# A graph-attention and residual-norm kernel: row maxima of every third chunk subtracted by an accumulating DMA, and the maxima written and read in another layout

## The chip, the cores and the metric

The kernel runs on one core of one Trainium2 chip. The metric is the device time of one execution in microseconds (us). Three executions of the kernel before took 1765.34, 1768.12 and 1771.2 us, median 1768.12 us. A fourth was recorded by the profiler; all rows below come from it. PE is TensorE, PEld its weight loads, DVE is VectorE, ACT is ScalarE, POOL is GpSimd, SP is SyncE; "SPq" and "POOLq" are the instructions with which these two start DMAs.

## What is computed

Eight graphs of 1500 nodes with 64 features pass through four layers, each followed by a residual addition and a layer norm. The change touches only the first layer, a graph attention with four heads:

```python
scores = jnp.einsum('hbnd,hbdm->hbnm', f_self, f_other)
masked = a_h * scores
masked = jnp.where(masked >= 0, masked, 0.2 * masked)
masked = masked / jnp.sqrt(jnp.float32(ATT))
masked = masked + jnp.where(a_h == 0, jnp.float32(-1000000000.0), jnp.float32(0.0))
attn = jax.nn.softmax(masked, axis=-1)
attn = attn * jnp.where(a_h == 0, jnp.float32(0.0), jnp.float32(1.0))
...
node_features = jnp.einsum('bhnm,bhmo->bhno', attn, feats)
```

The softmax needs the maximum over m of each row n, which is subtracted before the exponential. The other three layers multiply the adjacency matrix with the features (a mean over neighbours, a dense layer, a thresholded sum).

## The kernel before

**Units and chunks.** A graph's attention is cut into 6 units (2 pairs of heads times 3 slices of 500 rows n). In a unit the scores stand transposed, m on the partitions and n along the row, in 12 chunks (`STEPS`) of 125 partitions x 1000 numbers (two heads x 500 rows n). There are 48 units and 576 chunks. All engines walk through one common counter `q` of chunks, each executing what its list has for that `q`; semaphores hold them together.

**One chunk q.** PE fills a bank pair of the 3-deep ring `Z` with mask and scores (`fill_z`, lines 496 and 498), and may do so only when the ring's user three places earlier has been read. ACT applies the leaky slope and writes the chunk to the row store `LS` (`bend`, line 677), DVE folds it into the running maximum `RUN` straight from `Z` (`maximum`, lines 820 and 823). Since the maximum is known only when all 12 chunks are through, the rest follows `LAG` = 18 chunks later: chunk e = q - 18 gets its maxima subtracted, ACT exponentiates it at q = e + 20 (`expo`, line 685), and PE weighs it, two chunks at a time, at e + 22 (`weigh`, line 535).

**The subtraction.** Of each three chunks (`TURN`) POOL subtracts two (line 403) and DVE the third (line 837), as the last thing in DVE's list for that `q`. They take turns: before the first of its two, POOL waits on `sub_dve` until DVE has done the chunk before. POOL's list also has the loads of the adjacency matrix (line 365, a DMA that casts f32 to fp8), the power of the layer norms (408), the low halves (412) and the bases of the later layers (417, 420).

**The maxima's way.** At the unit's end PE transposes `RUN` (`turn_run`, line 509, eight transposes, each reading 125 columns of `RUN` with a stride of `ST` = 4 elements), DVE reduces (line 829), ACT applies the slope (line 692), SP writes 125 x 8 numbers to the HBM buffer `row_maxima` as 125 x 2 runs of 4 (line 303), waits for that, and reads them back, broadcast to 125 partitions of `MB` (line 309). `MB` has two halves, one per unit in turn.

**Layer norms and the later layers** of graph b - 1 run beside the attention of graph b: DVE has six larger operations a layer (among them lines 905, 909, 914 and 922), ACT squares and casts, PE multiplies the adjacency matrix (line 586) and turns the result back (line 596). After the last attention chunk these stages of graph 7 run alone.

## Time and profile before

| | |
|---|---|
| median of three executions | 1768.12 us |
| the profiled execution, whole | 1762.62 us |
| its span, first to last instruction | 1760.8 us |
| PE busy | 1454.2 us (83%) |
| DVE busy | 1384.5 us (79%) |
| ACT busy | 1241.6 us (71%) |
| POOL busy | 1089.5 us (62%) |
| mean granted clock of TensorE | 0.912 of 2.4 GHz |

The profiled execution took 5.5 us less than the median. The first read of the maxima starts at 89.0 us and the last at 1649.2 us, so 47 unit intervals take 1560.2 us, 33.2 us each, or 2.77 us a chunk; 89 us lie ahead of them and 112 us behind. In the profile, "idle before" an instruction is the time for which its engine stood still, and the name behind the arrow is what ended that. A mean busy time of a pipelined matmul is shorter than its own duration, because neighbours overlap.

### The profile page before, as it was taken

To read this page: it belongs to the slowest core of one execution; us is meant where nothing else is said; L and a number is where in the kernel's file an instruction comes from. 1 tells how busy PE (TensorE), PEld (TensorE's weight loads), DVE (VectorE), ACT (ScalarE), POOL (GpSimd) and SP (SyncE) were. 2 spreads that over 40 slices of the span, in tenths; PEclk is the share of its full clock that TensorE was granted. 3 is DMA by queue.
4 is the path that set the end of the run, shared out by engine and by line. 5 is a ranking of instruction groups with operands and counts; after the bars stand their busy time and mean duration, and the time that the engine had idled before them with its cause. 6 is when DMAs were issued, how large, how long until landed. Compare 5 with 4: busy or idle time off the path is not lost.

```text
span 1760.8 us, 22052 instructions
## 1 busy us (share of the span) xinstructions
PE 1454.2 (83%) x7728; PEld 718.8 (41%) x7728; DVE 1384.5 (79%) x1623; ACT 1241.6 (71%) x1475; POOL 1089.5 (62%) x581
## 2 busy tenths in 40 slices
PE   4487889898889889888889888988899987888745
PEld 3233334444444444444444443444444443344313
DVE  3567788878898778888888778987888788888654
ACT  2377878777687777777787777777687777777521
POOL 1056676676676666676576667776666766766642
PEclk9788989999899999999999999999999999999767
DMA  5413142122413133221522234130432214000000
GB/s 77 61 32 48 31 66 40 46 30 39 70 31 46 26 52 51 52 36 26 68 40 43 25 55 58 39 44 17 63 46 52 30 37 55 21 12 24 15 6 9
DMA packets 55067, 71.42 MB, mean 41 GB/s; under 512 B 21814, under 2 KB 42814, under 8 KB 54958
## 3 DMA queue, kind: packets, MB, share of 16 engines
q0 software_dynamic: 13824, 18.01, 13.7%
q1 hardware_dynamic: 41134, 52.01, 11.4%
q8 instruction: 62, 1.02, 0.3%
q14 instruction: 47, 0.39, 0.1%
HBM read 102.29 MB, written 3.26 MB: 60 GB/s over the span
## 4 chain that ended last, share of the span: by engine, by line
PE 45%; DVE 24%; issue 12%; ACT 11%; SPq 3%; POOL 3%; DMA 2%; ACTq 0%; POOLq 0%; DVEq 0%
PE M L586 11%; DVE RUN L823 9%; PE M L535 9%; PE Z L496 8%; PE Z L498 7%; ACT LS L677 6%; PE Z L509 4%; DVE LS L837 4%; ACT LS L685 3%; SPq L286 2%; DVE X L922 2%; POOL LS L403 2%; PE Z L596 2%; DVE RUN L820 2%; PE Z L657 2%
## 5 line engine op out<-in xcount | busy, mean ns | idle before, releaser
L403 POOL TENSOR_TENSOR LS<-LS,MB 125x1000 f32<-125x1000 f32 x384 | 894.7, 2346 | 489.4 <-DVE LS L837 334.8
L823 DVE TENSOR_TENSOR RUN<-Z,RUN 125x1000 f32<-125x1000 f32 x528 | 631.0, 1195 | 208.7 <-ACT LS L677 203.4
L677 ACT ACTIVATE LS<-Z 125x1000 f32<-125x1000 f32 x576 | 574.5, 998 | 262.0 <-PE Z L498 261.4
L685 ACT ACTIVATE LS<-LS 125x1000 f32<-125x1000 f32 x576 | 594.5, 1033 | 71.3 <-POOL LS L403 56.2
L496 PE MATMUL Z<-AT,BI 126*125 126x500 fp8e4 x1152 | 386.0, 418 | 140.1 <-DVE RUN L823 107.0
L535 PE MATMUL M<-LS,V 125*18 125x500 f32 x2304 | 326.7, 642 | 57.8 <-ACT LS L685 57.0
L498 PE MATMUL Z<-FS,FO 96*125 96x500 bf16 x1152 | 360.1, 395 | 0.0
L837 DVE TENSOR_TENSOR LS<-LS,MB 125x1000 f32<-125x1000 f32 x192 | 283.2, 1475 | 4.9 <-DMA MB<-row_maxima 2.8
L496 PEld LDWEIGHTS Z<-AT,BI 126*125 126x125 bf16 x1152 | 140.7, 146 | 282.9 <-DVE RUN L823 164.5
L498 PEld LDWEIGHTS Z<-FS,FO 96*125 96x125 bf16 x1152 | 165.5, 144 | 111.4 <-issue 21.3
L586 PE MATMUL M<-AT,XP 125*128 125x500 fp8e4 x756 | 206.8, 396 | 0.7 <-ACTq L735 0.7
L586 PEld LDWEIGHTS M<-AT,XP 125*128 125x128 f16 x756 | 63.6, 98 | 169.6 <-issue 106.8
L509 PE MATMUL Z<-ID,RUN 125*125 125x125 f32 x384 | 99.9, 407 | 26.8 <-DVE RUN L820 24.1
L535 PEld LDWEIGHTS M<-LS,V 125*18 125x18 f32 x2304 | 39.6, 98 | 185.4 <-issue 101.7
L509 PEld LDWEIGHTS Z<-ID,RUN 125*125 125x125 f32 x384 | 91.5, 323 | 46.3 <-DVE RUN L820 39.9
L365 POOL DMA_DIRECT2D A<-in_adj_dram x96 | 53.7, 560 | 85.9 <-PE Z L552 58.7
L820 DVE TENSOR_SCALAR RUN<-Z 125x1000 f32<-125x1000 f32 x48 | 57.3, 1193 | 47.8 <-DMA B<-in_L_gnn_bias_dram 30.0
L829 DVE TENSOR_REDUCE RMAX<-Z 125x8 f32<-125x1000 f32 x48 | 57.3, 1194 | 26.1 <-PE Z L509 26.1
L596 PEld LDWEIGHTS Z<-WW,YT 128*125 128x125 f32 x504 | 63.9, 190 | 28.7 <-issue 22.0
L922 DVE SCALAR_TENSOR_TENSOR X<-Y,RSTD 125x768 f32<-125x768 f32 x28 | 72.4, 2585 | 3.6 <-POOL RSTD L408 2.4
L596 PE MATMUL Z<-WW,YT 128*125 128x64 f32 x504 | 64.7, 272 | 3.7 <-DVE RUN L820 3.7
L552 PEld LDWEIGHTS Z<-ID,A 125*125 125x125 f32 x276 | 45.8, 215 | 53.5 <-issue 28.5
(118 smaller groups left out, 1039.6 us busy)
## 6 DMA issues: line engine op xcount, KB each, us to landing
MB<-row_maxima SPq DMA_DIRECT2D x48, 488.3 KB
A<-in_adj_dram POOLq DMA_DIRECT2D x96, 183.1 KB, 4.8
FO<-PARTS SPq DMA_DIRECT2D x192, 46.9 KB, 2.1
FS<-PARTS SPq DMA_DIRECT2D x192, 46.9 KB, 2.1
XP<-in_x_dram SPq DMA_DIRECT2D x8, 375.0 KB
XA<-in_x_dram SPq DMA_DIRECT2D x8, 375.0 KB
out_dram<-X SPq DMA_DIRECT2D x7, 375.0 KB
row_maxima<-LMAX SPq DMA_DIRECT2D x48, 3.9 KB
```

The source lines that it names most:

```text
L403: nc.gpsimd.tensor_tensor(rows, rows, MB[:, u % 2, :, :], ALU.subtract).then_inc(sub_pool, 1)
L496: nc.tensor.matmul(z[:P, hh, :], BI[:, :], AT[:, g % RS, quarter, :, k], start=True, stop=False)
L498: last = nc.tensor.matmul(z[:P, hh, :], FO[:, 2 * p + hh, m * P:(m + 1) * P], FS[:, 2 * p + hh, s * C:(s + 1) * C], start=False, stop=True)
L509: last = nc.tensor.transpose(z[:P, hh, c * P:(c + 1) * P], RUN[:, u % 2, hh, c:C:ST], ID[:P, :P])
L535: last = nc.tensor.matmul(M0[VW * n:VW * n + VC, 0:C], V[:, b % 2, e % STEPS, 2 * p + hh, :], LS[:P, e % RL, hh, :], start=(p == 1 and j = ...
L586: last = nc.tensor.matmul(M1[:, 0:C], XP[:, m, :], AT[:P, (NS * b + c) % RS, m // ST, :, m % ST], start=(m == 0), stop=(m == NT - 1))
L596: last = nc.tensor.matmul(z[:P, 0, k * F:(k + 1) * F], YT[:, k * P:(k + 1) * P], WW[:, 1 if l == 1 else 0, :], start=True, stop=True)
L677: nc.scalar.activation(LS[:P, q % RL, :, :], banks("Z", q)[:P], ACT.Prelu, alpha=0.2).then_inc(bent, 1)
L685: nc.scalar.activation(rows, rows, ACT.Exp, scale=0.25).then_inc(exps, 1)
L823: nc.vector.tensor_tensor(run, z, run, ALU.max).then_inc(maxed, 1)
L837: nc.vector.tensor_tensor(rows, rows, MB[:, u % 2, :, :], ALU.subtract).then_inc(sub_dve, 1)
L922: nc.vector.scalar_tensor_tensor(out=X[:, :, :], in0=Y[:, :, :], scalar=F ** 0.5, in1=RSTD[:, :].unsqueeze(2).to_broadcast(bc3), op0=ALU.m ...
```

## The change

Five things change.

1. Every third chunk (c % 3 = 2 within its unit) is no longer subtracted by DVE. POOL starts a DMA from `MB` to `LS` that accumulates (`accum_op=ALU.add`) for chunk e + 2 ahead of its own subtraction of chunk e, so 192 DMAs of 125 x 1000 f32 in all. ACT's `expo` of such a chunk waits for that DMA's semaphore, one of four (`BY_DMA`).
2. POOL keeps its two of three, and no longer waits for a turn.
3. ACT now makes the negative of the maximum (`scale=-0.2, alpha=5.0`), and both POOL and the DMA add it.
4. PE's transposes read `RUN` in contiguous blocks of 125 columns in place of every fourth column. The maxima then lie as (j i) and are written as 1000 pieces of one number, by two DMAs of 112 and 13 partitions.
5. `MB` has 128 partitions, and the broadcast read fills all 128.

```diff
-                sp.dma_start(spread[u % 2].rearrange("(h i c) -> i h c", i=P, c=ST),
-                             LMAX[:, u % 2, :].rearrange("p (h c) -> p h c", c=ST)).then_inc(max_out[u % 2], 16)
-                sp.wait_ge(max_out[u % 2], 16 * (u // 2 + 1))
+
+                for rows in (slice(0, 112), slice(112, P)):
+                    sp.dma_start(spread[u % 2].rearrange("(j i) -> i j", i=P)[rows], LMAX[rows, u % 2, :],
+                                 allow_slow_non_contiguous=True).then_inc(max_out[u % 2], 16)
+                sp.wait_ge(max_out[u % 2], 32 * (u // 2 + 1))
                 if u >= 2:
-                    sp.wait_ge(sub_pool, by_pool(STEPS * (u - 1)))
-                    sp.wait_ge(sub_dve, STEPS * (u - 1) // TURN)
+
+                    sp.wait_ge(exps, STEPS * (u - 1))
                 sp.dma_start(MB[:, u % 2, :, :].rearrange("p h c -> p (h c)"),
-                             spread[u % 2].partition_broadcast(P)).then_inc(mb_in[u % 2], 16)
+                             spread[u % 2].partition_broadcast(128)).then_inc(mb_in[u % 2], 16)
@@
                 if c == 0:
                     pool.wait_ge(mb_in[u % 2], 16 * (u // 2 + 1))
-                if e % TURN == 0:
-
-                    pool.wait_ge(sub_dve, e // TURN)
                 pool.wait_ge(bent, e + 1)
                 rows = LS[:P, e % RL, :, :]
-                nc.gpsimd.tensor_tensor(rows, rows, MB[:, u % 2, :, :], ALU.subtract).then_inc(sub_pool, 1)
+                nc.gpsimd.tensor_tensor(rows, rows, MB[:P, u % 2, :, :], ALU.add).then_inc(sub_pool, 1)
+
+            def subtract_by_dma(e):
+
+                u, c = divmod(e, STEPS)
+                pool.wait_ge(mb_in[u % 2], 16 * (u // 2 + 1))
+                pool.wait_ge(bent, e + 1)
+                if u:
+
+                    pool.wait_ge(exps, e - STEPS + 1)
+                pool.dma_start(LS[:P, e % RL, :, :].rearrange("p h c -> p (h c)"),
+                               MB[:P, u % 2, :, :].rearrange("p h c -> p (h c)"),
+                               accum_op=ALU.add).then_inc(sub_dma[c // TURN], 16)
@@
                 e = q - LAG
+                if 0 <= e < QN and e % TURN == 0:
+                    subtract_by_dma(e + TURN - 1)
                 if 0 <= e < QN and e % TURN != TURN - 1:
                     subtract(e)
@@
-                        last = nc.tensor.transpose(z[:P, hh, c * P:(c + 1) * P], RUN[:, u % 2, hh, c:C:ST], ID[:P, :P])
+                        last = nc.tensor.transpose(z[:P, hh, c * P:(c + 1) * P], RUN[:, u % 2, hh, c * P:(c + 1) * P], ID[:P, :P])
@@
                 if e % TURN == TURN - 1:
-                    act.wait_ge(sub_dve, e // TURN + 1)
+                    u, c = divmod(e, STEPS)
+                    act.wait_ge(sub_dma[c // TURN], 16 * (u + 1))
@@
-                nc.scalar.activation(LMAX[:, u % 2, :], RMAX[:, u % 2, :], ACT.Prelu, alpha=0.2).then_inc(max_bent, 1)
+                nc.scalar.activation(LMAX[:, u % 2, :], RMAX[:, u % 2, :], ACT.Prelu, scale=-0.2,
+                                     alpha=5.0).then_inc(max_bent, 1)
@@
-                e = q - LAG
-                if 0 <= e < QN and e % TURN == TURN - 1:
-                    subtract(e)
```

How the instructions stand on POOL before, at the passage from the second unit of subtractions to the third (`A` is the adjacency matrix, `LS` the row store, `MB` the maxima; a semaphore's name behind "waits" is what the instruction waits for):

```order
L365 DMA A<-in_adj_dram 125x1500 [waits a_turned]
L403 TENSOR_TENSOR LS<-LS,MB 125x1000 [waits bent,sub_dve]
L403 TENSOR_TENSOR LS<-LS,MB 125x1000 [waits bent]
L403 TENSOR_TENSOR LS<-LS,MB 125x1000 [waits bent,sub_dve,mb_in1]
L403 TENSOR_TENSOR LS<-LS,MB 125x1000 [waits bent]
L403 TENSOR_TENSOR LS<-LS,MB 125x1000 [waits bent,sub_dve]
L403 TENSOR_TENSOR LS<-LS,MB 125x1000 [waits bent]
```

The same place on POOL in the changed kernel:

```order
L368 DMA A<-in_adj_dram 125x1500 [waits a_turned]
L413 DMA LS<-MB 125x1000 [waits exps,bent,mb_in0]
L403 TENSOR_TENSOR LS<-LS,MB 125x1000 [waits bent] x2
L413 DMA LS<-MB 125x1000 [waits exps,bent,mb_in1]
L403 TENSOR_TENSOR LS<-LS,MB 125x1000 [waits bent,mb_in1]
L403 TENSOR_TENSOR LS<-LS,MB 125x1000 [waits bent]
L413 DMA LS<-MB 125x1000 [waits exps,bent,mb_in1]
```

POOL has one DMA start more per three chunks, and nothing there waits for DVE.

DVE before, through one unit, from its first fold into `RUN` after the slice's bookkeeping on:

```order
L823 TENSOR_TENSOR RUN<-Z,RUN 125x1000
L842 COPY AT<-Z 125x3x125
L829 TENSOR_REDUCE RMAX<-Z 125x8
L823 TENSOR_TENSOR RUN<-Z,RUN 125x1000
L837 TENSOR_TENSOR LS<-LS,MB 125x1000
L823 TENSOR_TENSOR RUN<-Z,RUN 125x1000 x3
L837 TENSOR_TENSOR LS<-LS,MB 125x1000
L823 TENSOR_TENSOR RUN<-Z,RUN 125x1000 x3
```

DVE at the same place in the changed kernel:

```order
L839 TENSOR_TENSOR RUN<-Z,RUN 125x1000
L852 COPY AT<-Z 125x3x125
L845 TENSOR_REDUCE RMAX<-Z 125x8
L839 TENSOR_TENSOR RUN<-Z,RUN 125x1000 x10
L836 TENSOR_SCALAR RUN<-Z 125x1000
```

The four subtractions are gone from the unit; the ten folds stand behind one another, and nothing else has moved.

## Rows read from the trace of the kernel before

**Rows 1.** The page's head: span; busy us, share and instructions of each engine.
```profile
span 1760.8 us, 22052 instructions
PE 1454.2 (83%) x7728; PEld 718.8 (41%) x7728; DVE 1384.5 (79%) x1623; ACT 1241.6 (71%) x1475; POOL 1089.5 (62%) x581
```
**Rows 2.** Busy time in one 200 us stretch: PE, PEld, DVE, ACT, POOL; clock; DMA share.
```profile
800.00:1000.00 200.00, 175.97 (x948) 87.12 (x948) 166.14 (x192) 151.97 (x182) 132.18 (x68) 0.93 0.28 44
```
**Rows 3.** Chain of work that ended last: shares of the span by engine, by line.
```profile
PE 45%; DVE 24%; issue 12%; ACT 11%; SPq 3%; POOL 3%; DMA 2%; ACTq 0%; POOLq 0%; DVEq 0%
PE M L586 11%; DVE RUN L823 9%; PE M L535 9%; PE Z L496 8%; PE Z L498 7%; ACT LS L677 6%; PE Z L509 4%; DVE LS L837 4%; ACT LS L685 3%; SPq L286 2%; DVE X L922 2%; POOL LS L403 2%; PE Z L596 2%; DVE RUN L820 2%; PE Z L657 2%
```
**Rows 4.** Waits, 400 to 1400 us: waiter <- awaited: us in total, times, longest.
```profile
POOL LS L403 <- DVE LS L837: 216.9, 82, 7.5
ACT LS L677 <- PE Z L498: 144.8, 89, 4.7
DVE RUN L823 <- ACT LS L677: 121.7, 165, 1.5
...
PE Z L496 <- DVE RUN L823: 69.1, 37, 5.8
...
PE Z L509 <- DVE RUN L820: 16.0, 10, 2.4
PE Z L552 <- DVE RUN L823: 8.8, 5, 2.0
...
ACT LS L685 <- POOL LS L403: 15.4, 15, 3.0
```
**Rows 5.** Costliest groups: count, busy us, mean ns of one, idle before and releaser.
```profile
L403 POOL TENSOR_TENSOR LS<-LS,MB 125x1000 f32<-125x1000 f32 x384 | 894.7, 2346 | 489.4 <-DVE LS L837 334.8
L837 DVE TENSOR_TENSOR LS<-LS,MB 125x1000 f32<-125x1000 f32 x192 | 283.2, 1475 | 4.9 <-DMA MB<-row_maxima 2.8
L509 PE MATMUL Z<-ID,RUN 125*125 125x125 f32 x384 | 99.9, 407 | 26.8 <-DVE RUN L820 24.1
...
L365 POOL DMA_DIRECT2D A<-in_adj_dram x96 | 53.7, 560 | 85.9 <-PE Z L552 58.7 <-PE M L552 23.3 <-issue 2.7
...
L552 PE MATMUL Z<-ID,A 125*125 125x125 f32 x276 | 56.7, 320 | 10.9 <-DVE RUN L823 10.6
```
**Rows 6.** Timeline of two unit ends: start us, duration us, engine, instruction, idle before.
```profile
801.39 2.17 PE L509 MATMUL Z<-ID,RUN 125*125 125x125 f32 x8 [0.32 <-DVE XA L867]
...
805.26 1.00 ACT L677 ACTIVATE LS<-Z 125x1000 f32<-125x1000 f32 x1 [3.88 <-PE Z L498]
...
841.38 0.49 PE L552 MATMUL Z<-ID,A 125*125 125x125 f32 x3
```
**Rows 7.** Timeline of a stretch without extra work: two slopes of ACT behind one another.
```profile
149.24 1.00 ACT L677 ACTIVATE LS<-Z 125x1000 f32<-125x1000 f32 x1
...
151.06 1.01 ACT L677 ACTIVATE LS<-Z 125x1000 f32<-125x1000 f32 x1
```
**Rows 8.** Timeline of SP: a write of the maxima and the read behind it.
```profile
675.10 0.25 SPq L303 DMA_DIRECT2D row_maxima<-LMAX  x1
677.22 0.26 SPq L309 DMA_DIRECT2D MB<-row_maxima  x1
```
**Rows 9.** Timeline of POOL: the first subtraction with what that read brought.
```profile
683.85 2.33 POOL L403 TENSOR_TENSOR LS<-LS,MB 125x1000 f32<-125x1000 f32 x1 [2.29 <-DMA MB<-row_maxima]
```
**Rows 10.** DMA queue of POOL: packets, MB, share of 16 engines; its issues and landing us.
```profile
q0 software_dynamic: 13824, 18.01, 13.7%
...
A<-in_adj_dram POOLq DMA_DIRECT2D x96, 183.1 KB, 4.8
```
**Rows 11.** Chain in order of time: two pieces that are reads of the maxima.
```profile
88.99 9.28 DMA MB<-row_maxima
...
241.26 8.81 DMA MB<-row_maxima
```

12 lines of the change are left out of this document (4 added, 8 removed).

## The prediction, made before the changed kernel ran

> **What bounds the kernel now.** I read the page's busy shares first. PE is the busiest with 83% of the span and DVE follows with 79% [rows 1]; neither is near the whole, so the engines wait for one another, and a share alone decides nothing. A 200 us stretch in the middle, about one graph, says the same with cleaner numbers: PE 176.0 us, DVE 166.1, ACT 152.0, POOL 132.2 [rows 2]. Second, the chain of work that ended last: PE has 45%, DVE 24%, ACT 11%, "issue" 12%, POOL and DMA 5% together. The removed DVE subtraction, line 837, has 4% of the chain, and the transposes of the running maximum, line 509, another 4% [rows 3]. Third, the waits between 400 and 1400 us. PE stands still for DVE for 69.1 + 16.0 + 8.8 = 93.9 us of these 1000. But DVE in turn waits 121.7 us for ACT's slope, and ACT 144.8 us for PE's scores. POOL waits 216.9 us for its turn behind DVE, and that hardly reaches anybody: ACT waits 15.4 us for POOL [rows 4]. So this is a ring PE, ACT, DVE with a 3-deep buffer. Where nothing else is to be done, its pace is ACT's: two slopes start 151.06 - 149.24 = 1.82 us apart [rows 7], against 2.77 us as the mean of a chunk. The other 0.95 us a chunk come from the extra work on DVE and PE, which comes in lumps. One lump stands at every unit's end: PE turns the running maximum for 2.17 us, and ACT gets no scores for 3.88 us [rows 6].
>
> **Part 1, the subtraction leaves DVE.** 192 instructions, 283.2 us busy, 1475 ns each [rows 5]; DVE's busy time should fall to 1384.5 - 283.2 = 1101 us. What of that lies on the path? From above: the chain's 4% of 1760.8 us, 70 us. Another ceiling, from the waits: PE waits for DVE 9.4% of the middle, over the 1560 us of the 47 unit intervals 146 us, all of which would have to vanish. From below: zero, since DVE itself waits 121.7 us in 1000 for ACT [rows 4], so in plain stretches the subtraction fills a hole that would be there anyway, and what it delays in lumps ACT or PE may hold up next. I take 45 us, two thirds of the chain's share, because the chain is the view that counts only what nothing else hid, and a part of it falls to the next in line, ACT at 1.82 us a chunk.
>
> **Part 2, POOL.** It loses the wait for turns and gains 192 DMA starts. The trace has no accumulating DMA. The nearest row is the start of an adjacency load, 560 ns [rows 5]: 192 x 0.56 = 108 us; twice that if an accumulation needs two reads to be described, 215 us. The turns were 334.8 us of POOL's waits [rows 5], and per unit of 33.2 us POOL is busy 132.2 / 200 x 33.2 = 21.9 us [rows 2]; with four starts 24 to 26.5. That cover holds down to units of 26.5 us, and I expect about 31.5. I put 0 on it. Beyond the cover the price is four starts per unit less the room, see the rivals. The starts have a wait for `bent` and one for `exps`, both for work that ACT did many chunks earlier, and one for `MB`, behind which POOL's two own subtractions and the adjacency loads queue; the subtraction of chunk 0 waited for `MB` at the same place before.
>
> **Part 3, does the DMA land in time?** POOL starts it at q = e + 16 of its list and ACT wants the chunk at e + 20, so 4 chunks of lead, 4 x 2.77 = 11 us, and at the faster pace still 10. The nearest row is the adjacency load: 4.8 us to landing [rows 10], for 125 rows of 6000 B read. The accumulation reads 4000 B of `MB` and 4000 B of `LS` per row, 8000 B, and writes 4000; by bytes read 4.8 x 8/6 = 6.4 us at most, and from below about 4.8 x 4/6 = 3.2 if the second read is free. At a unit's start the lead is shorter on POOL's side, but there ACT first wants POOL's chunks 0 and 1, two instructions of 2.35 us each, which come later than 4.7 us. I take 5.5 us and 0 on the path. Occupancy: the queue's share of 13.7% is 241 us over 96 loads, 2.5 us of all 16 engines each [rows 10]; four accumulations a unit at 2.5 to 5 us are 10 to 20 us on top of 28% of 33.2 = 9.3 [rows 2]. It fits.
>
> A rule of the Trainium skill (the page Collectives: The Full Stack, section The bandwidth ceiling: the fold count and why AG ≠ RS ≠ AR) speaks against this change: an addition in the DMA engines needs two source reads and two read descriptors on one ring, while a copy needs one. No row here shows an accumulation. By it the doubled occupancy, 5 us, would be the right one of the two, and the sum would stay as it is, but the first rival below would be nearer.
>
> **Part 4, contiguous transposes.** Line 509 has 384 transposes of 125x125 f32 reading with stride; line 552 has transposes of the same shape reading contiguously. Mean busy 99.9 / 384 = 260 ns against 56.7 / 276 = 205 ns [rows 5], 55 ns apart, 21 us in all; in the timeline at full clock 2.17 / 8 = 271 against 0.49 / 3 = 163 ns [rows 6], 108 ns apart, 41 us. They lie on the path in each unit, because ACT stands still behind them [rows 6]. I take 30 us, bounds 15 and 41.
>
> **Part 5, the way of the maxima.** The read of `MB` starts at 677.22 and POOL goes on at 683.85 [rows 8, 9], 6.6 us for 488 KB, although the adjacency load, which writes 183.1 KB and reads four times that, 732 KB, lands in 4.8 [rows 10]. With 128 partitions I expect it near that row or under it, 4 to 4.8 us: 1.8 to 2.6 us earlier. It can't be slower than now by more than the 3 rows added, 3/125 of 6.6 us. Of this only what POOL's lateness costs counts: the two reads in the chain, 9.28 and 8.81 us [rows 11], both while the pipeline fills, and the 15.4 us in 1000 of ACT behind POOL [rows 4]. I take 5 us. Against it stands the write: 2.1 us from its start to the read's [rows 8] for 250 pieces; 1000 pieces in two DMAs cost between one more start, 0.25 us, and four times as long, 6.4 us. SP has nothing queued behind it but the read. Between MB landing and ACT's need of chunk 0 there are six chunks, 16 us, less the write and read of 8.7 and a start and a subtraction of 2.9, some 5 us; so nothing of it is paid near the lower end, and I take that.
>
> The Trainium skill (DMA: Bandwidth & Descriptors, section Why a DMA increments its semaphore by 16 and not by 1) says that the number of DMA engines is the largest one up to 16 that divides the slowest dimension: 125 gives 5 with 25 rows each, 128 gives 16 with 8. The slow read of `MB` agrees with that [rows 9], though no row counts engines. By it the read's own moving would fall to about a third, and the sum would gain no more than the 5 us, since the path hardly passes there.
>
> **The clock.** In the middle 0.93 of 2.4 GHz is granted [rows 2], so about a seventh of the time runs at 1.2 GHz, often behind a stall of PE. Fewer stalls could give some of it back, at most 7% of PE's work; I put nothing on it and leave it to the lower end.
>
> **The sum.** 1762.6 (the profiled execution) - 45 - 0 - 0 - 30 - 5 = 1682.6 us. The median of the runs is 5.5 us above that execution, so 1688 us. Its own range, with part 1 between 0 and 110 and part 4 between 15 and 41, and 10 us of new waits: 1620 to 1750.
>
> **The rivals.**
> - **The accumulating DMAs clog the 16 engines (slower).** In a unit 33.2 us x (1 - 0.28) = 23.9 us are free [rows 2], 6 us for each of the four. Above 6 us of all engines per DMA, 2.4 times the adjacency load's 2.5 [rows 10], the queue falls behind, ACT waits for it in every unit, and the unit takes 9.3 us plus four DMAs. At 6.5 us that is 35.3 us, and 47 x 35.3 + 89 + 112 = 1860 us, less 10 for the ends. For it: the operation has no row, and the adjacency load already takes longer than its bytes need. Against it: the bytes read are only 8/6 of that row's. Chance 12%, near 1850 us.
> - **Starting an accumulation is dear on POOL (slower).** POOL's unit is 21.9 us and four starts. From (31.5 - 21.9) / 4 = 2.4 us a start on POOL sets the pace; at 3 us the unit is 33.9 us, 47 x 33.9 + 89 + 112 = 1794 us in all; at 3.5, near 1890. Against it: the one start in the trace takes 0.56. Chance 8%, near 1800 us.
> - **ACT and PE take it all (no change).** DVE's slack of 121.7 us in 1000 [rows 4] says that it isn't the bound; the transposes' gain is then lost in the ring too, or the longer write of the maxima eats it. 1762 to 1773 us, chance 10%.
> - **The ring runs free (much faster).** All of PE's waits for DVE go, 146 us, with the transposes 30 and the maxima 5: 1768 - 181 = 1587 us. For it: POOL stops making DVE wait too (line 837 has a mean of 1475 ns). Against it: ACT's own waits for PE, 144.8 us in 1000, and the dear layer-norm steps on DVE stay. Chance 13%, 1580 to 1620.
>
> **How the numbers follow.** Likeliest case 57%, 1688 us. A measurement of this kernel can tell 0.3%, about 5 us, from no change. Faster by more: 57 + 13 = 70% and a small part of the others, 0.71; within: 0.09; slower: 0.20. The range should leave out 2 in 10: it goes from 1610, which leaves out most of the free ring, to 1805, which takes in the dear start near its threshold and leaves out the clogged engines.
>
> **What would show it.** Right: DVE busy near 1100 us with no subtraction; the transposes at 1.3 to 1.6 us per eight; `MB` landing in 4 to 5 us; POOL's waits now for `MB` alone, its starts under 1.2 us; ACT's waits for the accumulation near zero; PE's waits for DVE down by a third or more. Wrong: a row in which the exponential waits for the DMA in most units, a DMA share above 0.8, starts on POOL above 2 us, or PE's waits for DVE as large as before with only the name of the DVE line changed, from line 823 behind a subtraction to line 823 behind ACT.

## The result

The changed kernel takes 2125.95 us, median of four executions (2121.59 to 2126.83). The kernel before, measured beside it, takes 1768.03 us. The ratio is 1.2019 (95% interval 1.1993 to 1.2045): the change costs 358 us, where 80 us less were forecast, and the time lies 321 us above the upper end of the range. The kernel before was measured again beside each experiment and took 1757.8 to 1760.9 us there; the ratios of the experiments are to that. Executions more than 1.5% above the fastest of the same kernel are left out of a ratio; of the experiments only e5 had such, two of ten.

The page's head of the changed kernel, which answers to [rows 1], and its DMA queues, which answer to [rows 10] (packets, MB, share of 16 engines):

```profile
span 2119.8 us, 22148 instructions
...
PE 1479.1 (70%) x7728; PEld 696.3 (33%) x7728; DVE 1304.9 (62%) x1431; ACT 1244.7 (59%) x1475; POOL 1235.2 (58%) x773
...
q0 software_dynamic: 41472, 114.02, 49.9%
q1 hardware_dynamic: 78958, 52.60, 11.9%
```

No engine is busier than 70%. PE and ACT do about their old work and DVE less, in a span that is 359 us longer: most of this is waiting. DVE has lost 192 subtractions of 283.2 us [rows 5], but its busy time fell by only 79.6 us, so something else on DVE has become longer by 204 us.

The stretch of [rows 2] (PE, PEld, DVE, ACT, POOL; clock; DMA share; GB/s), and the chain by engine and by line, which answers to [rows 3]:

```profile
800.00:1000.00 200.00, 147.11 (x781) 69.46 (x781) 140.49 (x139) 123.11 (x147) 123.42 (x74) 0.85 0.65 81
```
```profile
issue 35%; POOL 27%; PE 17%; DVE 10%; ACT 6%; DMA 2%; SPq 2%; POOLq 0%; ACTq 0%; DVEq 0%
POOL LS L403 18%; DVE RUN L839 4%; PE M L600 4%; ACT LS L691 4%; PE M L549 3%; POOL LS L413 3%; PE Z L510 3%; PE Z L512 2%; POOL RSTD L420 2%; POOL A L368 2%; DMA LS<-MB 2%; PE Z L671 1%; ACT LS L700 1%; SPq L287 1%; POOL XP L424 1%
```

POOL went from 3% of the chain to 27%, and "issue", time for which the profile has no cause, from 12% to 35%. The waits between 400 and 1400 us, as in [rows 4]:

```profile
DVE RUN L839 <- ACT LS L691: 291.6, 189, 12.2
POOL LS L413 <- DMA MB<-row_maxima: 223.2, 21, 29.3
ACT LS L691 <- PE Z L512: 172.5, 71, 14.6
ACT LS L700 <- POOL LS L403: 128.9, 28, 12.3
PE Z L510 <- DVE RUN L839: 128.3, 34, 14.5
...
ACT LS L700 <- DMA LS<-MB: 18.8, 6, 5.2
```

ACT waited 15.4 us for POOL before; now it waits 128.9, in 28 waits, and the 1000 us hold about 24 units. So the exponential waits for POOL about once a unit. The wait for the accumulating DMA itself is small, 18.8 us. The groups of the page that changed (busy, mean ns of one, idle before), and the landings in us:

```profile
L403 POOL TENSOR_TENSOR LS<-LS,MB 125x1000 f32<-125x1000 f32 x384 | 997.5, 2877 | 0.0
...
L413 POOL DMA_DIRECT2D LS<-MB x192 | 231.3, 1205 | 569.9 <-DMA MB<-row_maxima 501.8
...
L890 DVE TENSOR_TENSOR PARTS<-REST,PARTS 128x500 bf16<-128x500 f32 x21 | 138.7, 6606 | 0.0
...
L523 PE MATMUL Z<-ID,RUN 125*125 125x125 f32 x384 | 59.0, 301 | 53.9 <-DVE RUN L836 51.7
```
```profile
LS<-MB POOLq DMA_DIRECT2D x192, 488.3 KB, 7.1
MB<-row_maxima SPq DMA_DIRECT2D x48, 500.0 KB, 4.7
A<-in_adj_dram POOLq DMA_DIRECT2D x96, 183.1 KB, 6.9
```

Three things stand out. POOL's subtraction is 23% longer than in [rows 5], though the row misleads: the time from one pair of subtractions with its start to the next is 5.05 us at its shortest, 0.55 more than without the start (e5 and e7 below). The transposes did get cheaper (59.0 us against 99.9), and `MB` lands in 4.7 us. And a DVE instruction that touches neither maxima nor ring, the low part of the features, takes 6606 ns on average. It had 1117 ns before.

### The profile page after: what moved, and what is told of

It is laid out like the page before. It is cut to its first block, busy times and chain, and to the rows that moved or that the text cites. A ratio compares the mean times of both kernels' runs of the same rounds, so it can differ in the third digit from the quotient of the medians.

```text
span 2119.8 us, 22148 instructions
## 1 busy us (share of the span) xinstructions
PE 1479.1 (70%) x7728; PEld 696.3 (33%) x7728; DVE 1304.9 (62%) x1431; ACT 1244.7 (59%) x1475; POOL 1235.2 (58%) x773
## 3 DMA queue, kind: packets, MB, share of 16 engines
q1 hardware_dynamic: 78958, 52.60, 11.9%
## 4 chain that ended last, share of the span: by engine, by line
issue 35%; POOL 27%; PE 17%; DVE 10%; ACT 6%; DMA 2%; SPq 2%; POOLq 0%; ACTq 0%; DVEq 0%
POOL LS L403 18%; DVE RUN L839 4%; PE M L600 4%; ACT LS L691 4%; PE M L549 3%; POOL LS L413 3%; PE Z L510 3%; PE Z L512 2%; POOL RSTD L420 2%; POOL A L368 2%; DMA LS<-MB 2%; PE Z L671 1%; ACT LS L700 1%; SPq L287 1%; POOL XP L424 1%
## 5 line engine op out<-in xcount | busy, mean ns | idle before, releaser
L839 DVE TENSOR_TENSOR RUN<-Z,RUN 125x1000 f32<-125x1000 f32 x528 | 632.3, 1198 | 601.8 <-ACT LS L691 597.8
L403 POOL TENSOR_TENSOR LS<-LS,MB 125x1000 f32<-125x1000 f32 x384 | 997.5, 2877 | 0.0
L413 POOL DMA_DIRECT2D LS<-MB x192 | 231.3, 1205 | 569.9 <-DMA MB<-row_maxima 501.8
L600 PE MATMUL M<-AT,XP 125*128 125x500 fp8e4 x756 | 219.5, 416 | 6.0 <-ACTq L751 5.9
L368 POOL DMA_DIRECT2D A<-in_adj_dram x96 | 73.3, 773 | 139.5 <-PE Z L566 114.6
L890 DVE TENSOR_TENSOR PARTS<-REST,PARTS 128x500 bf16<-128x500 f32 x21 | 138.7, 6606 | 0.0
L533 PE MATMUL M<-AT,DS 125*18 125x500 fp8e4 x288 | 30.5, 546 | 119.9 <-ACT O L714 119.9
L420 POOL TENSOR_TENSOR RSTD<-RSTD,NHALF 125x12 f32<-125x12 f32 x28 | 66.9, 2389 | 78.0 <-DVE RSTD L926 77.8
L932 DVE SCALAR_TENSOR_TENSOR X<-Y,RSTD 125x768 f32<-125x768 f32 x28 | 95.9, 3424 | 3.6 <-POOL RSTD L420 2.4
L523 PE MATMUL Z<-ID,RUN 125*125 125x125 f32 x384 | 59.0, 301 | 53.9 <-DVE RUN L836 51.7
L523 PEld LDWEIGHTS Z<-ID,RUN 125*125 125x125 f32 x384 | 50.7, 206 | 73.5 <-DVE RUN L836 65.2
L610 PEld LDWEIGHTS Z<-WW,YT 128*125 128x125 f32 x504 | 63.1, 188 | 27.5 <-issue 20.8
```

The costliest lines, as they stand in the source:

```text
L368: pool.dma_start(A8[:, t % RA, :], adj_v[b, s, k]).then_inc(a_in[t % RA], 16)
L403: nc.gpsimd.tensor_tensor(rows, rows, MB[:P, u % 2, :, :], ALU.add).then_inc(sub_pool, 1)
L413: pool.dma_start(LS[:P, e % RL, :, :].rearrange("p h c -> p (h c)"), MB[:P, u % 2, :, :].rearrange("p h c -> p (h c)"), accum_op=ALU.add). ...
L523: last = nc.tensor.transpose(z[:P, hh, c * P:(c + 1) * P], RUN[:, u % 2, hh, c * P:(c + 1) * P], ID[:P, :P])
L600: last = nc.tensor.matmul(M1[:, 0:C], XP[:, m, :], AT[:P, (NS * b + c) % RS, m // ST, :, m % ST], start=(m == 0), stop=(m == NT - 1))
L839: nc.vector.tensor_tensor(run, z, run, ALU.max).then_inc(maxed, 1)
```

## Two readings of the trace

**DVE is shut out.** The timeline of DVE and then that of POOL over the same 24 us of the changed kernel (start, duration):

```profile
1122.65 1.20 DVE L839 TENSOR_TENSOR RUN<-Z,RUN 125x1000 f32<-125x1000 f32 x1 [1.12 <-ACT LS L691]
1123.76 20.36 DVE L890 TENSOR_TENSOR PARTS<-REST,PARTS 128x500 bf16<-128x500 f32 x1
```
```profile
1125.73 1.74 POOL L429 TENSOR_TENSOR Y<-X,RDEN 125x768 f32<-125x768 f32 x1
1127.14 1.14 POOL L413 DMA_DIRECT2D LS<-MB  x1
1127.72 5.16 POOL L403 TENSOR_TENSOR LS<-LS,MB 125x1000 f32<-125x1000 f32 x2
1132.26 1.41 POOL L413 DMA_DIRECT2D LS<-MB  x1
1132.83 5.39 POOL L403 TENSOR_TENSOR LS<-LS,MB 125x1000 f32<-125x1000 f32 x2
1137.31 1.71 POOL L413 DMA_DIRECT2D LS<-MB  x1
1137.89 5.68 POOL L403 TENSOR_TENSOR LS<-LS,MB 125x1000 f32<-125x1000 f32 x2
```

L890 stands for 20.36 us and ends at 1144.12. POOL's unbroken row of instructions ends at 1137.89 + 5.68 = 1143.57, 0.55 us earlier, and L890 needs 0.67 us when nothing disturbs it. The folds into `RUN` (L839) have one operand in PSUM and keep their 1.20 us in the middle of such rows; L890 has two in SBUF. The Trainium skill (SBUF — State Buffer, section Who interferes with whom) says that a DVE instruction with two SBUF inputs contends with a GpSimd instruction that reads SBUF. Of another case, DVE's 2-port modes, it says that the engine that was first keeps the shared pair for its whole instruction. The trace agrees on who is hit. It shows more: the loser waits not for one instruction of POOL (2.3 us), but for its whole row. The end is always the same: all six of the long ones here end 0.55 us behind POOL's last instruction. In e7 and e18 below, where a DMA start or nothing follows POOL's last subtraction, they end 0.54 us behind that subtraction (342.32 and 341.78 us; 714.20 and 713.66). All 21 of them, with the least, median and longest ns:

```profile
L890 DVE TENSOR_TENSOR PARTS<-REST,PARTS x21: 668/672/21755, 97.6 to 1625.2; 128x500 bf16<-128x500 f32 x21
```

14 of the 21 take under 700 ns, so this is not a slower instruction. It meets a closed door now and then.

**The way of the maxima is a loop.** A unit's maxima are bent by ACT, written and read back by SP, subtracted by POOL from chunk 0 and then awaited by ACT's exponential of chunk 0. After six more chunks ACT comes to the next bend. So a unit takes that way plus six chunks, if the exponential waits at its end. I took both from the timelines of every kernel, as means over the 48 units (the way starts at the end of the bend): from bend to write, from write to read, from read to the start of POOL's subtraction of chunk 0, the whole way from bend to exponential, the unit, the rest (unit less way), and in how many units the exponential starts less than 1 us behind POOL's chunk 0. The last column adds up, over all DVE instructions but its own subtraction, what each took above the least of its group (same line, same tiles, same shape): about the time for which DVE was held.

| kernel | bend to write | to read | to POOL | way | unit | rest | waits at its end | DVE held |
|---|---|---|---|---|---|---|---|---|
| before | 0.70 | 2.40 | 8.25 | 14.3 | 33.2 | 18.9 | 36 | 60 |
| after | 1.91 | 9.24 | 5.69 | 19.5 | 40.8 | 21.3 | 48 | 266 |
| e1 | 0.94 | 7.95 | 5.15 | 16.8 | 34.9 | 18.1 | 48 | 58 |
| e5 | 0.68 | 2.60 | 8.47 | 14.5 | 33.0 | 18.5 | 38 | 122 |
| e7 | 0.36 | 2.45 | 9.38 | 15.0 | 35.7 | 20.8 | 48 | 242 |
| e6 | 2.74 | 3.20 | 9.12 | 17.7 | 38.1 | 20.4 | 48 | 217 |
| e2 | 1.79 | 3.20 | 8.61 | 16.3 | 39.6 | 23.3 | 48 | 330 |
| e12 | 0.25 | 4.07 | 7.59 | 15.4 | 35.1 | 19.7 | 32 | 145 |
| e10 | 0.03 | 2.29 | 7.24 | 13.5 | 32.2 | 18.7 | 21 | 50 |
| e13 | 0.03 | 2.35 | 6.95 | 13.7 | 32.0 | 18.3 | 14 | 90 |
| e14 | 0.03 | 2.26 | 7.30 | 13.6 | 31.5 | 17.9 | 20 | 42 |

47 units that are 7.55 us longer are 355 of the 358 us. 5.2 of the 7.55 are in the way, 2.3 in the rest. DVE was held for 206 us more, about the 204 us that its busy time had too much. And before the change the exponential already followed POOL's chunk 0 within 1 us in 36 of 48 units. Part of this was in the waits of the kernel before, in two rows over the whole span that I had not put beside its 48 units:

```profile
POOL LS L403 <- DMA MB<-row_maxima: 150.6, 34, 9.8
...
ACT LS L685 <- POOL LS L403: 56.2, 39, 7.0
```

Of ACT's 39 waits 25 are at chunk 0 of a unit, the other 14 at later chunks. In 11 more units ACT came to chunk 0 just as POOL was done, or within 1 us of it, and shows no wait.

## Experiments: the maxima's way and its transposes

**e1**: the kernel before with the change's maxima way alone (contiguous transposes, 1000 pieces, `MB` of 128 partitions).

```diff
-        MB = sb("MB", [P, 2, 2, C], f32)
+        MB = sb("MB", [128, 2, 2, C], f32)
...
-                sp.dma_start(spread[u % 2].rearrange("(h i c) -> i h c", i=P, c=ST),
-                             LMAX[:, u % 2, :].rearrange("p (h c) -> p h c", c=ST)).then_inc(max_out[u % 2], 16)
+                for rows in (slice(0, 112), slice(112, P)):
+                    sp.dma_start(spread[u % 2].rearrange("(j i) -> i j", i=P)[rows], LMAX[rows, u % 2, :],
+                                 allow_slow_non_contiguous=True).then_inc(max_out[u % 2], 16)
...
-                             spread[u % 2].partition_broadcast(P)).then_inc(mb_in[u % 2], 16)
+                             spread[u % 2].partition_broadcast(128)).then_inc(mb_in[u % 2], 16)
...
-                        last = nc.tensor.transpose(z[:P, hh, c * P:(c + 1) * P], RUN[:, u % 2, hh, c:C:ST], ID[:P, :P])
+                        last = nc.tensor.transpose(z[:P, hh, c * P:(c + 1) * P], RUN[:, u % 2, hh, c * P:(c + 1) * P], ID[:P, :P])
```

> The kernel before with parts 4 and 5 of the change alone: contiguous transposes, maxima written as 1000 pieces of one number by two DMAs, MB on 128 partitions. DVE keeps its subtraction and POOL its turns. Theory A (the piecewise write is the main loss: in the changed kernel SP waits 7 to 13 us from the write's start to the read's, even 9.0 us in the first unit where no accumulating DMA has run): the write takes 8 to 9 us against 2.1, POOL starts each unit about 5 us late and the time is 1900 to 2000 us. Theory B (the accumulating DMAs and POOL's unbroken trains are the loss, and the write is slow only because their packets stand ahead of it): the write takes 2 to 4 us, and the time is 1720 to 1770 us.

1849.5 us, 1.0509 (1.0473 to 1.0544). SP of e1, a write and the read behind it, which answers to [rows 8]:

```profile
708.86 0.87 SPq L305 DMA_DIRECT2D row_maxima<-LMAX  x2
717.26 0.34 SPq L311 DMA_DIRECT2D MB<-row_maxima  x1
```

8.40 us against 2.12, and in the mean over the units 7.95 against 2.40. So this part, from which the prediction expected a gain of 35 us, alone costs 90. The time lies below the first theory's 1900 us: POOL starts not 5 us late but 2.5 in the mean of the way, since the faster read gives 3.1 back. In the changed kernel the first unit shows the same, ahead of any accumulation: the write at 86.12, the read at 95.10.

**e4**: `MB` of 128 partitions alone.

```diff
-        MB = sb("MB", [P, 2, 2, C], f32)
+        MB = sb("MB", [128, 2, 2, C], f32)
...
-                             spread[u % 2].partition_broadcast(P)).then_inc(mb_in[u % 2], 16)
+                             spread[u % 2].partition_broadcast(128)).then_inc(mb_in[u % 2], 16)
```

> The kernel before with one edit, MB on 128 partitions and the broadcast read filling them. In the changed kernel that read lands in 4.7 us (median) against 6.6 before. Read at 4 us and 0 to 15 us gained: 1753 to 1768 us. If the read's lateness was never on the path, 1768 us within 0.3%.

1728.1 us, 0.9812 (0.9784 to 0.9840). `MB` lands in 4.1 us in place of some 6.6, and that gives 32 us, twice the most that was expected.

**e10**: e4, and SP starts each of the two blocks of 24 feature loads of a graph behind the maxima's write and read of that unit, not ahead of them.

```diff
-                if r == 1 and 1 <= b < B:
+                if r == 2 and 1 <= b < B:
...
-                if r == 37 and b + 1 < B:
+                if r == 38 and b + 1 < B:
```

> MB on 128 partitions as in e4, and SP's two blocks of 24 feature loads a graph placed behind the write and read of the maxima of the same position in its list, not ahead. Theory P: in e4 two of six units start the write 1.7 to 2.7 us late behind these loads; that goes, 2 x 2 us a graph at most, 8 graphs: 10 to 35 us below e4, 1695 to 1720 us. If the path isn't the pace there: 1728 us as e4.

1714.6 us, 0.9759 (0.9722 to 0.9795), the fastest kernel here that computes the same in the same places. The two waits from before:

```profile
ACT LS L685 <- POOL LS L403: 24.7, 23, 3.6
POOL LS L403 <- DMA MB<-row_maxima: 17.8, 9, 6.8
```

150.6 us of waiting for `MB` have become 17.8. POOL now has another wait ahead of chunk 0: in 31 units it stands still and starts within 0.2 us of the end of DVE's subtraction, its turn, with `MB` landed before (the page calls most of this "issue").

**e11**: e4 with the write split into two DMAs of 112 and 13 rows, in runs of four as before.

```diff
-                sp.dma_start(spread[u % 2].rearrange("(h i c) -> i h c", i=P, c=ST),
-                             LMAX[:, u % 2, :].rearrange("p (h c) -> p h c", c=ST)).then_inc(max_out[u % 2], 16)
+                for rows in (slice(0, 112), slice(112, P)):
+                    sp.dma_start(spread[u % 2].rearrange("(h i c) -> i h c", i=P, c=ST)[rows],
+                                 LMAX[rows, u % 2, :].rearrange("p (h c) -> p h c", c=ST)).then_inc(max_out[u % 2], 16)
```

> e4 with the maxima written by two DMAs of 112 and 13 partitions, as in the changed kernel, but in runs of four numbers (250 pieces). It parts the piecewise write into its two edits. If the pieces are the cost (1000 of one number): write to read stays 2.2 to 2.6 us and the time is 1725 to 1740 us. If the second DMA is: write to read 5 us or more and over 1790 us.

1726.0 us, 0.9829 (0.9798 to 0.9860), the same as e4. So the second DMA costs nothing that can be measured; the 1000 pieces do.

**e14**: e10 with contiguous transposes and the write still in runs of four. The maxima then stand at permuted places of their unit's rows, so rows are reduced by the maximum of another row; the work is the same.

```diff
-                        last = nc.tensor.transpose(z[:P, hh, c * P:(c + 1) * P], RUN[:, u % 2, hh, c:C:ST], ID[:P, :P])
+                        last = nc.tensor.transpose(z[:P, hh, c * P:(c + 1) * P], RUN[:, u % 2, hh, c * P:(c + 1) * P], ID[:P, :P])
```

> e10 with contiguous transposes, but the maxima still written in runs of four and read back in that order, so that the maxima stand at permuted rows (left out: their right order). It has the transposes' gain without the piecewise write. My prediction's part 4 took 30 us (15 to 41): 1674 to 1700 us, PE's eight transposes at 1.1 in place of 2.1 us. If the transposes aren't on the path: 1715 us.

1680.2 us, 0.9563 (0.9528 to 0.9598), 34 us below e10. The eight transposes at a unit's end, PE at full clock:

```profile
654.40 1.11 PE L509 MATMUL Z<-ID,RUN 125*125 125x125 f32 x8
```

1.11 us against 2.17 [rows 6]. From this an estimate of what the pieces alone cost, e1 less e14 less the 13 us between e4 and e10, if these parts add up: 1849.5 - 1680.2 - 13.4 = 156 us.

**e8** and **e16** look for a way to have both, contiguous transposes and a short write. e8 is e4 and stores `RUN` in blocks, so that DVE reads and writes it with a stride and PE reads it without:

```diff
-        RUN = sb("RUN", [P, 2, 2, C], f32)
+        RUN = sb("RUN", [P, 2, 2, ST, P], f32)
...
-                run, z = RUN[:, u % 2, :, :], banks("Z", q)[:P]
+                run = RUN[:, u % 2, :, :, :].rearrange("p h c i -> p h i c")
+                z = banks("Z", q)[:P].rearrange("p h (i c) -> p h i c", c=ST)
```

> The kernel before with MB on 128 partitions and the running maximum stored in four blocks of 125 columns, which DVE writes with a stride, so that PE's transposes read contiguously while the write of the maxima keeps its runs of four. PE's eight transposes take 1.1 us in place of 2.1, 48 times: 30 to 45 us less than MB128 alone, 1683 to 1700 us, if DVE's strided writes are as fast as before (1195 ns). If these are slower, DVE's line 823 shows it and the time is over 1728 us.

1887.6 us, 1.0737 (1.0699 to 1.0775), 160 us above e4. The fold of each chunk is 63% longer:

```profile
L824 DVE TENSOR_TENSOR RUN<-Z,RUN 125x1000 f32<-125x1000 f32 x528 | 1029.9, 1951 | 66.7 <-ACT LS L677 47.9 <-DVE REST L876 0.2
```

e16 (e10 and the contiguous reads) turns the reduced maxima once more on PE, to 8 rows of 125, which are written as 8 runs. Beside what is shown, `LMAX` moves to 8 other partitions, and the place in PE's ring is free only behind ACT's bend, not behind DVE's reduction:

```diff
+                nc.tensor.transpose(banks("RT", u)[0:8, 0, 0:P], RMAX[:, u % 2, :], ID[:P, :P]).then_inc(max_turned, 1)
...
-                nc.scalar.activation(LMAX[:, u % 2, :], RMAX[:, u % 2, :], ACT.Prelu, alpha=0.2).then_inc(max_bent, 1)
+                nc.scalar.activation(LMAX[:, u % 2, :], banks("RT", u)[0:8, 0, 0:P], ACT.Prelu, alpha=0.2).then_inc(max_bent, 1)
```

> e10 with contiguous transposes and the maxima in their right rows without the piecewise write: behind DVE's reduction PE turns the 125 x 8 maxima once more into 8 x 125, ACT applies the slope to these, and SP writes 8 runs of 125 numbers. It uses e14's gain in a kernel that computes the whole. Theory P: the write stays at 2 to 2.5 us, PE has one small transpose more per unit, and the ring's place of the maxima is free a little later: 1680 to 1700 us. If PE's extra step waits for DVE in its list (a stall of a microsecond or more a unit), 1715 us or more.

1746.5 us, 0.9916 (0.9888 to 0.9943): 32 us slower than e10, a miss. From write to read it has 1.60 us in the mean (1.22 the median) in place of 2.29, but from read to POOL 8.64 in place of 7.24, so the way is 14.3 us, 0.8 longer than e10's. POOL hardly waits for `MB` (twice), which lands in 3.7 us. As in e10 it starts chunk 0 within 0.2 us of the end of DVE's subtraction in 31 units, but all its waits ahead of chunk 0 add up to 105.9 us in place of 63.5, so the turn comes later. Why DVE comes later there is open; the longer use of PE's ring was not tried alone.

## Experiments: the subtraction

These five have the old maxima way (write in 250 runs, `MB` of 125 partitions). e5, e7, e6 and e2 make a ladder up to the changed kernel, and e3 stands beside e5.

**e5**: DVE's subtraction left out with no replacement (192 of 576 chunks are not reduced by their maximum); POOL keeps its turns, now behind a mark that DVE sets at the old place.

```diff
                 if 0 <= e < QN and e % TURN == TURN - 1:
-                    subtract(e)
+                    dve.sem_inc(dve_turn, 1)
...
                 if e % TURN == 0:
-                    pool.wait_ge(sub_dve, e // TURN)
+                    pool.wait_ge(dve_turn, e // TURN)
...
-                    act.wait_ge(sub_dve, e // TURN + 1)
+                    act.wait_ge(bent, e + 1)
```

> The run before with every third chunk left unsubtracted (192 of 576 subtractions left out), but now DVE counts up a semaphore at the place in its list where its subtraction stood, and POOL waits for it ahead of every second subtraction, as it did for the subtraction itself. Theory S (shut out: DVE's instructions with two SBUF operands get in only when POOL pauses, and the turns were such pauses): its lines like the bf16 low half fall back to about 1.1 us each from 3.4, and the time falls below the kernel before, to 1680 to 1740 us, 50 to 110 us under the run without turns. Rival L (POOL running ahead is harmless; the run without turns is slow by another order of DMAs or clock): within 10 us of the run without turns.

1768.9 us, 1.0026 (0.9995 to 1.0058). The ten executions lie between 1751.6 and 1781.8 us. To take 283 us of work from an engine and put it nowhere is worth nothing that can be measured, where 20 to 80 us were expected. DVE's other instructions were held for 122 us in place of 60, presumably because its subtraction no longer parts POOL's rows.

**e3**: the same without turns.

```diff
-                if e % TURN == 0:
-                    pool.wait_ge(dve_turn, e // TURN)
```

> The kernel before in which every third chunk isn't subtracted at all (left out: the subtraction of 192 of 576 chunks, so the exponentials of these are of another number), and POOL doesn't wait for turns. It has the relief of DVE without any DMA in its place. My prediction's part 1 said that this is worth 45 us of at most 146: 1660 to 1725 us. If DVE's relief is worth nothing because ACT and PE set the pace: 1755 to 1775 us. If POOL without turns shuts DVE out by itself, slower than before, over 1780 us.

1795.4 us, 1.0201 (1.0146 to 1.0256). Less work and fewer waits, and 26 us slower than e5, half of the least that was expected of the turns, from two executions 14 us apart. The low part of the features is held here too (its mean is 2.1 us in e5):

```profile
L876 DVE TENSOR_TENSOR PARTS<-REST,PARTS 128x500 bf16<-128x500 f32 x21 | 72.3, 3443 | 0.0
```

**e7**: e5 with the 192 accumulating DMAs started as in the change, each of 16 numbers a row in place of 1000 (so nearly all of the third is still left out). With them come what the change has around them: POOL adds the negated maxima, the starts and the read of `MB` wait for ACT's exponentials of earlier units, and ACT waits for the DMA. The start:

```diff
+                pool.dma_start(LS[:P, e % RL, 0, 0:16],
+                               MB[:P, u % 2, 0, 0:16],
+                               accum_op=ALU.add).then_inc(sub_dma[c // TURN], 16)
```

> As e6, but each DMA adds only 16 of 1000 numbers a partition (left out: the subtraction of the other 984 in every third chunk). The same 125 rows are described, a sixtieth of the bytes moved. If POOL's cost of starting and describing is what the DMA costs: within 15 us of e6 and POOL's starts at 1.1 to 1.2 us as before. If the bytes or the landing are: 60 us or more below e6, near e5.

1887.2 us, 1.0726 (1.0677 to 1.0774): 118 us above e5 for starts and next to no bytes, and 114 below e6: neither of the two expectations was the whole. DVE is held for 120 us more than in e5. The DMAs land in 2.5 us:

```profile
LS<-MB POOLq DMA_DIRECT2D x192, 7.8 KB, 2.5
```

**e6**: the whole accumulation, with turns.

```diff
-                pool.dma_start(LS[:P, e % RL, 0, 0:16],
-                               MB[:P, u % 2, 0, 0:16],
+                pool.dma_start(LS[:P, e % RL, :, :].rearrange("p h c -> p (h c)"),
+                               MB[:P, u % 2, :, :].rearrange("p h c -> p (h c)"),
```

> The accumulating DMA with the maxima's way of before, as in e2, with the turns kept by DVE's mark. Theory S: the held DVE instructions fall from 10.6 us to 1 to 3 us each, and the time from 2064 to 1790 to 1880 us; it stays above the kernel before because each DMA start costs POOL 1.2 us of its own and, by the lengthened subtractions (2874 against 2346 ns, two per start), another 1.1 us, so POOL's unit is 21.9 + 4 x 2.3 = 31 us. Rival D (the DMAs' traffic or landing is the loss): it stays above 1980 us.

2001.2 us, 1.1374 (1.1316 to 1.1432): 114 us more for the bytes, so the second of the two expectations held. The bytes are not paid by DVE, which is held for 217 us, and for 242 in e7. They are paid in the way of the maxima (17.7 us against 15.0), and most of that ahead of the write: 2.74 us against 0.36, because SP, which has the feature loads to start first, takes longer for each beside the accumulations: 0.94 us in the mean of the 384, with 0.60 in e7. SP in the changed kernel, one graph's loads and the write behind them:

```profile
1000.52 8.91 SPq L287 DMA_DIRECT2D FO<-PARTS  x6
1009.48 10.94 SPq L287 DMA_DIRECT2D FS<-PARTS  x6
1020.46 3.77 SPq L287 DMA_DIRECT2D FO<-PARTS  x6
1024.28 4.42 SPq L287 DMA_DIRECT2D FS<-PARTS  x6
1028.79 1.35 SPq L306 DMA_DIRECT2D row_maxima<-LMAX  x2
```

Six starts took 3.75 us before the change; here they take up to 10.94, and the maxima are written 28 us after the first.

**e2**: e6 without turns, that is the change with the old maxima way.

```diff
-                if e % TURN == 0:
-                    pool.wait_ge(dve_turn, e // TURN)
```

> The changed kernel with the maxima's way of before: strided transposes, write as 250 runs of four by one DMA, MB on 125 partitions. What is left of the change is the accumulating DMA and POOL without turns. Theory A: most of the loss is gone, 1720 to 1850 us. Theory B: it stays slow, 1950 to 2100 us, with DVE's instructions that read two SBUF operands held for over 10 us in places, as its line 890 was held for up to 21.8 us in the changed kernel.

2064.0 us, 1.1727 (1.1692 to 1.1763), 63 us above e6, and this row has grown from e6's 91.9 us to:

```profile
L889 DVE TENSOR_TENSOR PARTS<-REST,PARTS 128x500 bf16<-128x500 f32 x21 | 222.6, 10602 | 0.0
```

**What the ladder adds up to**, from the 1760 us of the kernel before in these runs (in another order the steps could come out otherwise): 9 (e5) + 118 (starts) + 114 (bytes) + 63 (turns gone) + 62 (maxima way, the change less e2) = 366 us, the change's 2126. The last term holds the gains of the transposes and of the wider `MB` beside the loss by the pieces. It is uncertain by some 8 us, since the kernel before took 1768 us beside the change and 1760 beside e2.

**e17 and e18: what the starts cost.** The gap from one pair of POOL's subtractions to the next is at its shortest 4.50 us in e5 and 5.05 in e7, so a start takes 0.55 us of POOL. 192 of those are 106 us, which POOL could fit into its idle time, and yet 118 us were lost. e17 makes the same starts, into a buffer that nobody reads, in the kernel before, with DVE's subtraction and its turns in place. e18 is e7 with 21 waits on POOL, which let DVE's low part through.

e17, against the kernel before, without the set-up of `SCR` and of its semaphores:

```diff
+            def beside(e):
...
+                pool.dma_start(SCR[:, k % 2, :], MB[:, u % 2, 0, 0:16],
+                               accum_op=ALU.add).then_inc(by_side[k % 2], 16)
...
+                if 0 <= e < QN and e % TURN == 0:
+                    beside(e)
                 if 0 <= e < QN and e % TURN != TURN - 1:
                     subtract(e)
```

> The kernel before, with DVE keeping its subtraction of every third chunk and with all turns; POOL starts 192 accumulating DMAs more, each of 16 numbers a row, from MB into a small buffer that nobody reads, at the places of the change's starts. Nothing is left out. Question: the same 192 starts took 118 us when DVE's subtraction was left out. If what they cost is their time on POOL and in the way of the maxima, they cost it here too, and more, since POOL's turn now passes through DVE: 1840 to 1890 us. If they cost by lengthening POOL's unbroken trains, during which DVE can't run an instruction with two operands in SBUF, DVE's own subtraction breaks the trains here, its longest excess stays under 3 us, and the starts cost little: 1765 to 1800 us.

e18, against e7:

```diff
                 if 0 <= e < QN and e % TURN != TURN - 1:
                     subtract(e)
+                b, r = graph_at(q + 1)
+                if r in MIDDLES and b + 1 < B:
+                    pool.wait_ge(lo_ready, NS * (b + 1) + MIDDLES[r] + 1)
```

> The kernel of e7 (192 accumulations of 16 numbers, so most of every third chunk's subtraction is left out; turns kept; 1887 us) with one thing more: 21 times POOL waits, one chunk ahead in its list, until DVE has done the low parts of the features (PARTS from REST and PARTS, the instruction that took 6.0 us on average there). If DVE's being shut out by POOL's trains is what the starts cost, that row falls from 126 us to 25 to 45, and the time by 40 to 90 us, to 1800 to 1850. If the long row is only a symptom and POOL's lateness is the cost, the wait makes POOL later still: 1885 to 1920 us.

e17: 1785.6 us, 1.0162 (1.0127 to 1.0197). The 192 starts cost 28 us when DVE's subtraction stands between POOL's pairs. DVE was still held longer than I had written: its low parts took up to 3.9 us, its own subtraction up to 6.3, 5.1 above its least where under 3 were named. e18: 1815.9 us, 1.0314 (1.0276 to 1.0353), 71 us below e7 by adding waits. The low parts of the two (least, median and longest ns), first e7, then e18:

```profile
L892 DVE TENSOR_TENSOR PARTS<-REST,PARTS x21: 665/8391/10791, 97.4 to 1445.8; 128x500 bf16<-128x500 f32 x21
```
```profile
L895 DVE TENSOR_TENSOR PARTS<-REST,PARTS x21: 668/2431/5074, 97.8 to 1385.4; 128x500 bf16<-128x500 f32 x21
```

Had POOL's lateness been the cost, the waits of e18 would have added to it. So some 71 of the 118 us come of DVE being held, and the starts with DVE's subtraction between them cost 28; the 19 us left are not separated. The starts alone do little (e17), the missing subtraction alone does little (e5); together they leave POOL's rows without gaps. The low parts' row fell from 126 to 47 us, just above the 45 named; DVE's holding in all from 242 to 182, since other steps met the door in their place.

## Experiments: repairs

**e12**: e6 with `MB` of 128 partitions and the feature loads behind the maxima (the diffs of e4 and e10).

> The accumulating DMA with turns kept by DVE's mark as in e6, MB on 128 partitions, maxima written in runs of four, and the feature loads behind the maxima. In e6 the write starts 2.7 us late on average (up to 11.7) because the feature loads' starts take SP 1.5 us each beside the accumulating DMAs' traffic. Theory P: that goes, 2.7 us a unit, and 1 to 2 us from the read: 48 x 4 = 190 us at most, so 1810 to 1920 us; still slower than before, since POOL's starts and lengthened subtractions (e7 against e5, 118 us) stay. If bytes hit elsewhere: over 1950 us.

1851.2 us, 1.0539 (1.0491 to 1.0587). 150 us better than e6 and still 5% slower than before: neither this nor e15 makes the accumulation pay.

**e13**: e12 without any accumulation, that is e10 with every third subtraction left out and turns by mark (the diff of e5 on e10).

> e10 (MB on 128 partitions, feature loads behind the maxima) with every third chunk left unsubtracted (192 of 576 subtractions left out) and the turns kept by DVE's mark. With the maxima's way no longer the pace in half of the units, DVE's relief could show: if it is worth what my prediction's part 1 took, 45 us, 1660 to 1680 us. If ACT and PE set the pace in the rest, as e5 suggests (no gain over the kernel before), within 10 us of 1715. If freed POOL and DVE get into each other's way more than the relief brings, over 1725.

1696.0 us, 0.9644 (0.9599 to 0.9689). Against e10 it says what DVE's relief is worth where the maxima's way is short: 19 us, between the 35 or more of one expectation and the 10 at most of the other. Against e12 it says what the accumulation costs there: 155 us.

**e15**: e12 with the DMA started behind POOL's subtraction of chunk e, so that `MB`'s first use is not delayed.

```diff
-                if 0 <= e < QN and e % TURN == 0:
-                    subtract_by_dma(e + TURN - 1)
                 if 0 <= e < QN and e % TURN != TURN - 1:
                     subtract(e)
+                if 0 <= e < QN and e % TURN == 0:
+                    subtract_by_dma(e + TURN - 1)
```

> e12 with one edit: POOL starts the DMA for chunk e + 2 behind its own subtraction of chunk e, not ahead of it, so that chunk 0 of a unit isn't held by the start. Theory P: the start (1.13 us) and the longer first subtraction (0.3 us) leave the path, 47 x 1.4 = 66 us at most: 1785 to 1835 us. If the later start makes ACT wait for the DMA (7 us to landing) instead: over 1860 us, with a row of ACT's exponential waiting for it in most units.

1898.1 us, 1.0799 (1.0748 to 1.0851), 47 us worse. ACT now meets the DMA itself, in 54 waits, where e12 has 12:

```profile
ACT LS L702 <- DMA LS<-MB: 67.2, 54, 2.9
ACT LS L702 <- POOL LS L405: 59.9, 59, 3.9
```

**e9**: the kernel before with `LAG` = 16 in place of 18, so that the exponential wants its chunk two positions earlier (the row store, `LAG + 6` deep, shrinks with it).

```diff
-LAG = 18
+LAG = 16
```

> The kernel before with LAG = 16 in place of 18 (and RL = 22 row buffers): the first subtraction of a unit is due two chunks earlier. Theory P (the maxima's way is a loop with no slack: a unit is the path from ACT's slope of the maxima to the exponential of the unit's first chunk, 14.3 us, plus the list positions outside it, 18.9 us for six in the kernel before): two positions more stand outside the path, at 2.4 us or more each, so units of 36 to 38 us against 33.2 and a time of 1890 to 1990 us. Rival (my prediction's reckoning: some 5 us of slack ahead of the first chunk): nearly no change, 1755 to 1790 us.

1950.4 us, 1.1103 (1.1051 to 1.1156). The way is 13.1 us, shorter than before, but now eight chunks lie outside it, and the exponential waits in all 48 units (36 before). Two chunks fewer of lead cost 192 us in a kernel where only the depth of the row store changed with it. The unit grew by 3.95 us, of the 5.5 that two mean chunks take, so an estimate of the slack is 1.6 us in the mean at most. This is the most direct evidence that the way had hardly any.

## Why the prediction was wrong

**What bounds the kernel: half right.** The ring PE, ACT, DVE was read as the bound, and the second loop, through SP, HBM and POOL, was dismissed because ACT waited only 15.4 us in 1000 for POOL [rows 4]. The size of a wait doesn't say how near two loops are. Its count said more: the same row has 15 waits in a window of 30 units, and 13 of them are at chunk 0. When two loops are nearly level, both must shrink for a gain, and either may grow for a loss.

**Part 1, DVE's relief, mis-sized.** 45 us were taken, 0 (e5) and 19 (e13) measured. Both lie inside the stated 0 to 146; the lower bound's reason, a hole that is there anyway, was the right one. The chain's share was a poor guide: in e5 DVE's share of the chain fell from 24% to 12% and the time didn't fall with it.

**Part 2, POOL: the step that failed with the largest sum.** The part put 0 on the path for 192 starts and no turns; the ladder has 118 + 63 = 181 us. The start was put at 0.56 us of POOL, and it is 0.55. The 1.2 us in the row of L413 overlap the next subtraction. But the part sized only what POOL would lose, and counted the turns as a wait that hardly reaches anybody. They, and DVE's subtraction itself, were the gaps in which DVE got its two-operand instructions through. The row that pointed there was line 837 with a mean of 1475 ns, against 1195 for a fold of the same size; the prediction used it only as a hope for the free ring. What the change took from that side: 71 to 90 of the 118 us of the starts (e18, e17), and 63 for the turns.

**Part 3, does the DMA land in time: nearly right, and beside the point.** It lands in 7.1 us (6.3 at least), above the 6.4 taken as the most. With 10 us of lead ACT still waited only 36.2 us for it in all. Its occupancy, estimated with the adjacency loads at their old 241 us, is (0.499 x 2119.8 - 241) / 192 = 4.3 us of all 16 engines, inside the 2.5 to 5 taken. The rule of the page Collectives: The Full Stack in the Trainium skill (section The bandwidth ceiling: the fold count and why AG ≠ RS ≠ AR), two source reads for an addition, would have given 5 as an estimate: the trace is nearer to it than to a copy. "It fits" was true of the engines and false of the others in line: the feature loads' starts on SP, and the maxima behind them, which cost 114 us where the part put 0.

**Part 4, the transposes: right.** 30 us predicted, 34 measured (e14 against e10), 1.11 us for eight, which is under the 1.3 to 1.6 named.

**Part 5, the maxima's way: the step that failed first.** The reckoning "six chunks, 16 us, less 8.7 and 2.9, some 5 us slack" took the mean chunk of 2.77 us for these six, and one unit's 8.7 + 2.9 = 11.6 us for a way whose steps take 0.70 + 2.40 + 8.25 + 2.35 = 13.7 in the mean. In 36 units the exponential came within 1 us of POOL, so there was hardly any slack. Whatever the write took more, between +0.25 and +6.4 us, was therefore to be paid in good part, and the prediction took the lower bound. Measured from write to read: 7.95 us in the mean without accumulation (e1) and 9.24 with it, where it was 2.40, so +5.5 to +6.8. The same error made the gain of the wider `MB` small: 5 us taken, 32 measured (e4). The net was put at 5 us gained. e1 lost 90 with the transposes' 34 gained in it, so this part lost 124, if the two add up. The estimate of 156 us for the pieces is 3.3 us a unit, of the 5.5 that they took. The page DMA: Bandwidth & Descriptors in the Trainium skill says, in its section Rules for kernel authors, that a last dimension that is not contiguous becomes one descriptor per element. The trace agrees: q1 has 78958 packets in e1, and 42958 in e11, which has the same two DMAs in runs of four: 750 more for each of 48 writes.

**The clock** was put at nothing. The mean granted share fell from 0.912 to 0.842, and rose to 0.935 in e10 and 0.942 in e14: it moves with the waits. PE was busy for 25 us more; what part of the 358 us that is was not separated.

**The rivals.** Clogged engines: its threshold, 6 us of all engines per DMA, was not reached, and ACT waited only 36.2 us for the DMA, though the bytes did cost 114 us by SP's queue. Dear starts: its threshold, 2.4 us on POOL, was not reached either. "The longer write eats it", one clause of the rival that ended at no change, was true, but that rival put the whole at no change. The free ring was out of reach: e13, with no subtraction in its place at all, is at 1696. The rivals stood at 1850 and 1800 us, the dear start at 1890 at the most, each by one mechanism alone; here several come together: the pieces, the starts, the bytes and the missing turns.

**The signs.** Right: `MB` at 4.7 us, ACT's small waits for the accumulation (36.2 us in 13 waits), POOL waiting for `MB` (501.8 us of the 569.9 ahead of its starts). Nearly right: the transposes, and the start's row with 1.21 us for under 1.2. Wrong: DVE at 1304.9 us in place of 1100, and PE's waits for DVE, 128.3 us in the 1000 where it had 69.1.

## What to carry to other kernels

Before a transfer on a loop through memory is made longer, count the periods in which the consumer is just in time or waits at its end; if it is most of them, there is hardly any slack, however small the sum. Ask of every wait that is taken away which other engine used the pause, above all between DVE and POOL when both read two operands from SBUF. The cheap gains here were in the loop itself: a broadcast over 128 partitions and a queue that lets the maxima go first, 44 us together, without the change.

## What the runs showed of the hardware

- A DVE instruction with two SBUF inputs waits for the end of an unbroken row of POOL instructions, and not for one of them: up to 21.8 us for one of 0.67, ending 0.54 us behind POOL's last subtraction (the changed kernel, e7, e18). One with an input in PSUM isn't held (1.18 to 1.20 us, 528 folds).
- Starting an accumulating DMA takes 0.55 us of POOL between two others (4.50 us from pair to pair in e5, 5.05 in e7); its row shows 0.83 to 1.78, which runs on beside the next subtraction.
- 488 KB accumulated from SBUF to SBUF land in 7.1 us (median) and take, as an estimate, 4.3 us of all 16 engines; 7.8 KB land in 2.5 us.
- From the start of a write of 1000 pieces of 4 bytes to the read that waits for it are 7.95 us in the mean (e1; 6.5 to 12.2), of 250 pieces of 16 bytes 2.40 (the kernel before; 1.7 to 3.7).
- A broadcast read of the maxima into 128 partitions lands in 4.1 us (median, e4); POOL goes on 6.7 us after the start of one into 125 (median of the 34 units that wait for it before the change).
- DVE reading and writing f32 with a stride of 500 bytes takes 1951 ns (e8) for what takes 1195 without.
- A DMA start on SP takes 0.61 us in the mean of the 384 feature loads before the change and 0.94 beside POOL's accumulations (e6); stretches of six have up to 1.8 us each in the changed kernel.
